# Multiplying the identity into an unread bank at the start of three attentions

## The reference

```python
x = x + tanh(g_xattn[l]) * xattn_l(layernorm(x), ctx)
x = x + tanh(g_ffn[l]) * ffn_l(layernorm(x))
# xattn_l, l = 1..3: q = x Wq + bq; k, v = ctx Wk + bk, ctx Wv + bv, by heads
# softmax(q k^T / 4) v, then Wo, bo.  Layer 0 has no projections, but a mask.
```

## Time and profile before

| | us |
|---|---|
| median of 3 runs | 1578.96 |
| lowest, highest | 1573.89, 1581.24 |
| the profiled execution, its own time | 1582.87 |
| its span, first to last instruction | 1581.1 |
| TensorE busy in it | 1334.4 (84%) |
| VectorE busy | 966.2 (61%) |
| mean granted TensorE clock | 0.920 |

### The profile page before, as it was taken

How to read it: one execution, slowest core, us unless ns; L and a number is a source line. 1 busy time by engine, 2 the same in 40 slices (tenths; PEclk the granted TensorE clock), 3 DMA queues, 4 the chain that set the end, 5 groups by cost and what they waited for, 6 DMA issues and landing times.

```text
span 1581.1 us, 29388 instructions
## 1 busy us (share of the span) xinstructions
PE 1334.4 (84%) x9497; PEld 967.6 (61%) x9524; DVE 966.2 (61%) x2651; ACT 861.4 (54%) x1718; POOL 722.0 (46%) x835
## 2 busy tenths in 40 slices
PE   1798889997999489999999699838999488995985
PEld 1455479854566279999986356627887245565433
DVE  6789753435795743333337489574554277877797
ACT  3366854433787145555536388535565255785564
POOL 4557330105641577777641473257994426523000
PEclk9999999996899699999999699968999797897998
DMA  9999120079970333343247997024544499930001
GB/s 296 289 135 138 12 97 1 27 234 189 113 85 1 107 124 121 118 137 131 71 151 257 227 133 83 14 81 134 159 133 170 159 269 161 120 45 1 0 14 40
DMA packets 142064, 188.86 MB, mean 119 GB/s; under 512 B 21168, under 2 KB 107824, under 8 KB 141872
## 3 DMA queue, kind: packets, MB, share of 16 engines
q0 software_dynamic: 79936, 105.19, 38.8%
q1 hardware_dynamic: 61984, 81.79, 16.1%
HBM read 128.17 MB, written 50.20 MB: 113 GB/s over the span
## 4 chain that ended last, share of the span: by engine, by line
PE 66%; DVE 13%; DMA 7%; ACT 5%; issue 5%; POOL 2%; another core or an unknown queue 0%; SPq 0%; ACTq 0%; DVEq 0%; POOLq 0%
PE PS L1191 10%; PE PS L1211 10%; PE PS L987 9%; PE PS L1032 9%; PE PS L991 3%; PE PS L1203 3%; DMA stack<-qk_parts 2%; PE PS L1069 2%; DMA qk_parts<-q_parts 2%; PE PS L1005 2%; PE PS L873 2%; PE PS L1045 2%; PE PS L1012 1%; PE PS L859 1%; DVE act L2572 1%
## 5 line engine op out<-in xcount | busy, mean ns | idle before, releaser
L2087 DVE TENSOR_REDUCE nm<-PS 128x2 f32<-128x512 f32 x384 | 250.4, 677 | 56.5 <-PE PS L987 55.7
L987 PE MATMUL PS<-stack 48*128 48x256 f32 x1024 | 221.7, 344 | 49.4 <-issue 15.9
L987 PEld LDWEIGHTS PS<-stack 48*128 48x128 f32 x1024 | 158.9, 214 | 137.9 <-issue 71.6
L991 PE MATMUL PS<-stack 49*128 49x256 f32 x1024 | 211.0, 331 | 0.9 <-ACT probs L1512 0.6
L1211 PE MATMUL PS<-weights,hh 128*128 x936 | 189.9, 292 | 3.8 <-DVE hl L2414 3.7
L1191 PE MATMUL PS<-weights,xh 128*128 x468 | 171.3, 421 | 10.7 <-DVE xl L2398 4.6
L662 POOL DMA_DIRECT2D stack<-mt x128 | 71.6, 559 | 227.0 <-ACT mt L1521 225.2
L1512 ACT ACTIVATE probs<-PS 128x512 f32<-128x512 f32 x256 | 145.1, 595 | 52.7 <-PE PS L991 24.0
L1512 ACT ACTIVATE xng<-PS 128x512 f32<-128x512 f32 x256 | 145.3, 595 | 28.4 <-PE PS L1012 14.9
L1211 PEld LDWEIGHTS PS<-weights,hh 128*128 128x128 f32 x936 | 152.7, 193 | 5.9 <-issue 5.5
L991 PEld LDWEIGHTS PS<-stack 49*128 49x128 f32 x1024 | 149.2, 203 | 10.1 <-ACT probs L1512 4.8
(11 more groups left out here) (329 smaller groups left out, 3091.6 us busy)
## 6 DMA issues: line engine op xcount, KB each, us to landing
stack<-qk_parts POOLq DMA_DIRECT2D x128, 256.0 KB, 4.9
qk_parts<-stack SPq DMA_DIRECT2D x32, 512.0 KB, 6.9
qk_parts<-q_parts SPq DMA_DIRECT2D x32, 512.0 KB, 9.5
stack<-qk_parts POOLq DMA_DIRECT2D x128, 128.0 KB, 4.1
weights<-W_dram POOLq DMA_DIRECT2D x12, 1024.0 KB
wide<-ctxT_dram SPq DMA_DIRECT2D x16, 512.0 KB, 7.7
wslot<-y_tokens SPq DMA_DIRECT2D x16, 512.0 KB, 7.5
weights<-W_dram POOLq DMA_DIRECT2D x12, 512.0 KB
```

What stands on the lines that cost most here:

```text
L987: mm = pe.matmul(PS[:, u % 3, to], nat_q[:, at], nat_k, start=True, stop=True)
L991: mm = pe.matmul(PS[:, 3 + v % 3, to], key_k[:, at], key_q, start=(l > 0 or half == 0), stop=(l > 0), skip_group_check=(l == 0))
L2087: nc.vector.tensor_reduce(nm[:, j % 2, at:at + 2], PS[:, (2 * t + h) % 3, :].rearrange("p (q n) -> p q n", q=2), AX.X, ALU.max, negate=Tru ...
```

## The change

In front of the attentions of layers 1 to 3 TensorE waits until the third group's query remainder has been taken (so that banks 6 and 7 have been read), and then multiplies the identity by 512 columns of `wproj` four times, into bank 7. Behind the scores of each of the first 16 units it does the same with 128 columns, once. Nothing reads the result, and nothing waits for it.

```diff
+FILLED = 16
...
             def attend(l):
 
+                if l:
+                    pe.wait_ge(qlo_done, GROUPS * (l + 1) - 1)
+                    idle(512, 4)
                 for n in range(QUADS + BACK):
                     for m in range(2):
                         units = [4 * n + 2 * m + h for h in range(2)]
                         keyed = [u - LAG for u in units]
                         for u, v in zip(units, keyed):
                             scores(l, u if u < HEADS * B else None, v if 0 <= v < HEADS * B else None)
+                            if l and u < FILLED:
+                                idle(P, 1)
...
+            def idle(n, times):
+
+                for _ in range(times):
+                    pe.matmul(PS[:, 7, 512 - n:], ident[:], wproj[:, 3].rearrange("p c n -> p (c n)")[:, 0:n], start=True, stop=True)
```

## The result

| | before | after |
|---|---|---|
| median, us | 1580.1 (4 runs) | 1599.2 (4 runs) |
| lowest, highest | 1573.9, 1583.5 | 1594.0, 1602.0 |
| profiled execution, its own time | 1582.9 | 1594.0 |
| mean granted clock in it | 0.920 | 0.929 |

The account below looks back on a forecast made before the run. It took TensorE's low clock at the attention starts of layers 1 to 3 as the loss: -8.6 us if held, -6.0 with layer 1 midway, -4.8 after late rows, 3 on the median: 1576 us, range 1567 to 1588.

Parts of the forecast that it names:

- The clock: Attention starts, layers 1 to 3: full at the first score, then held in layers 2 and 3, open in layer 1.
- the gap before unit 13: TensorE's wait for the first row of maxima, forecast to shrink to 1.4, 0.8 and 0 us in layers 1 to 3.
- the head: Four 512-column multiplications before the first score: 3.45 us, hidden in layers 1 and 3, first score 0.9 us later in layer 2.
- Units 13 to 19: Stage up to the first times-V block: 4.3 us with the clock held, gaining 0.8, 0.7 and 1.0 us.
- The unit: Each of units 0 to 15 with its filler: 0.76 us at full clock, 1.34 at low, over VectorE's 0.60.
- The neighbours: Steps around each score with a filler behind it: 0.23 us to its second half, 0.22 to the filler.
- The row: First row of maxima, issued 1.0, 2.2 and 1.0 us later; half counted as cost: 0.5, 1.1 and 0.5 us.
- The first reading: First row's transfer hangs on what is queued ahead, so it lands when it did: cost 0.
- a fixed latency: Other case for the first row's transfer: the whole shift of its issue counts, 1.0, 2.2 and 1.0 us.
- The low stretch behind the front: Low-clock time from the first times-V block on: 5.1, 1.6 and 1.5 us gained in layers 1 to 3 if held.
- The slower one: Rival: clock falls just behind unit 12 in every layer, units 13 to 15 cost 1.34 us each; 7.5 us, 1586; chance 0.17.
- the full gain: Rival: clock holds everywhere at the attention starts, little given back; -8.6 us or more, about 1570; chance 0.27.

Follow-up runs that it names:

- Experiment 5: Changed kernel with one 512-column bf16 multiplication as each filler and 26, 12, 20 of them before layers 1, 2, 3: 1573.66 us, ratio 0.998.
- experiment 3: Changed kernel with one bf16 multiplication of 512 columns replacing each float filler behind units 0 to 15, leading multiplications kept: 1587.96 us, ratio 1.0072.
- Experiment 8: Changed kernel with the same float fillers set in twos behind every second unit: 1577.24 us, ratio 1.0014.
- Experiment 1: Changed kernel without the fillers behind units 0 to 15, the four 512-column multiplications in front kept: 1576.0 us, ratio 1.0032.
- experiment 7: Changed kernel with fillers behind units 0 to 7 only, in place of sixteen units: 1583.19 us, ratio 1.0055.
- experiment 10: Changed kernel with bf16 multiplications: 26, 12, 20 in front, two behind every second unit to 11, twelve behind unit 12: 1568.13 us, ratio 0.9953.

## Why the prediction was wrong

**The clock (the step that failed).** The prediction says: "I take the clock as full when the first score starts", and lets it fall, if at all, in the gap before unit 13. It was full at the first score, and it fell under the fillers, 0.5, 5.5 and 5.4 us later, with TensorE busy without a pause from the first score on. In layer 1 the prediction's own figures warned of it: the head was to leave 4.85 - 3.45 = 1.4 us idle ahead of the first score and left 1.74, more than the 1.67 behind which it had seen the clock fall, but it asked this of the gap before unit 13 alone. In layers 2 and 3 no gap explains the fall; there the fillers, taken as work that holds the clock, did not hold it. How much hangs on it can be worked out. With the measured unit of 0.85 us and the clock held, units 0 to 12 with their three transposes take 13 x 0.85 + 0.33 = 11.4 us in place of 11.0, 10.8 and 9.6, gap included: 2.8 us more over three layers. They took 18.1 more. So, by this estimate, 15.3 of the stage's 18.1 us are the low clock. Units 13 to 19 add 6.2 where 2.5 were to be gained, for the same cause. Experiment 5, where the clock held in two of the three fronts, bears it out by taking back 24.7 us, 4.8 of them by its cheaper filler; within experiment 3 the one front that kept the clock took 18.3 us and the two that lost it 29.2 and 28.0.

**The unit (mis-sized term).** 0.76 us was forecast, 0.85 measured; at the low clock 1.34 and 1.44. The 0.11 us between two full-row instructions was read from back transposes, which are single instructions; the two halves of a float multiplication start 0.21 us apart at the full clock and 0.37 at the low one; at the full clock that is the whole of the miss. The term was small: 13 x 0.09 = 1.2 us a layer at the full clock, 0.10 us a unit at the low one. The prediction's estimate by the Trainium skill (TensorE: Matmul & The Clock Gate, What overlaps and what doesn't) was 0.86, and the trace agrees with it, at 0.85, though no run here separates the second weight load from the rest of its instruction.

**The neighbours (a term not seen).** A score was given 0.23 us for its second half and 0.22 to the filler, with no word of what it loses by no longer following another score. Experiment 8 prices that at 0.31 us of the 0.85. In the forecast's sum it was hidden in steps read from a stretch where single scores alternate with full-row work, so the sum came near; what it hid is that another order of the same instructions stays under VectorE's pace. The Trainium skill (same page and section) says that a weight load overlaps running multiplications only where their row groups differ. That full-row fillers shut the scores off from each other agrees with it, since a filler uses all rows: 0.85 us a unit with a filler behind each, 0.54 with two behind a pair.

**The row.** Forecast: issued 1.0, 2.2 and 1.0 us later, 0.9 of layer 2's being the head. Measured against the first score: 4.6, 1.7 and 1.3 us later. The 4.6 are the low clock of layer 1, and the 1.7 and 1.3 of layers 2 and 3 stand near the 1.3 and 1.0 of the forecast. Whether the landing moves with the issue, the prediction left open and took half; the DMA times settle it. Layer 1's first row, before and after:

```profile
DMA to landing us min/median/max: 6.4/6.4/6.4
...
DMA to landing us min/median/max: 1.7/1.7/1.7
```

In layers 2 and 3 it took 6.5 and 5.0 us before, 5.5 and 4.5 after. So it landed 10.9, 10.7 and 9.6 us behind the first score before, and 10.9, 11.4 and 10.4 after: the landing moved by 0, 0.7 and 0.8 us where the issue moved by 4.6, 1.7 and 1.3. The first reading (it hangs on what is queued ahead) is nearer than a fixed latency. None of it cost anything, as the row was there before TensorE reached unit 13 in all three layers.

**The low stretch behind the front.** Forecast for a held clock: 5.1, 1.6 and 1.5 us gained. It stayed low for 1.7, 3.4 and 6.6 us behind the first times-V block in place of 12.45, 3.78 and 3.75; 8.2 us less at 2.06 us in 5.00 are 3.4 us gained, by estimate, far less than the fillers cost.

**The head.** Right: near enough hidden in layers 1 and 3 (0.3 us more, 0.5 less), and 0.9 us later in layer 2 (3.96 us from the last query instruction to the first score, 3.09 before). Experiment 1 shows that it costs the fronts nothing and gains little.

**The rivals.** The slower one had the kind right (fillers that run at the low clock) and the place and size wrong: not behind unit 12 but from the first to the seventh unit on, and 25 us in the fronts in place of 7.5. The rule of the Trainium skill in the full gain (same page, Why this matters for your kernels), that TensorE kept busy reaches the full clock, did not hold here: layer 1 was busy for 27.82 of 27.82 us at a granted clock of 0.51. The prediction had set the 12.45 us busy and low of the earlier trace rows against that rule, and then let the fillers hold the clock anyway.

**What stays open.** Which property of the work lets the clock fall is not settled, and each kernel has one profiled execution. Where TensorE had not been idle ahead of the first score, single float fillers lost the clock 5.4 to 5.9 us behind it (layers 2 and 3 of the change, layer 2 of experiment 7), a transpose after 6.0, bare scores after 4.8 and 5.7. Single bf16 fillers held it through all 16 units in layer 2 of experiment 3 and layers 1 and 3 of experiment 5, and lost it after 10.6 us in layer 2 of experiment 5. Float fillers in pairs held it through units 0 to 12 in layers 2 and 3 of experiment 8, but not in layer 1, with 1.82 us idle ahead. The length of a gap doesn't decide alone either: the prediction had 0.98 us (stayed) and 1.67 (fell), but the clock fell behind 1.07 us in layer 1 of experiment 10 and stayed behind 1.36 us in layer 3 of experiment 5. Nor do the runs settle why the steady stage behind the fronts was faster in some executions.

## What to carry to other kernels

Before filler work is set between real instructions, take its unit cost at the low clock as well as at the full one, and ask who paces the stage: a filler that fits under VectorE's 0.60 us a unit costs nothing, one of 0.85 costs a little (by the estimate above 2.8 us over three layers), and the same one at 1.44 cost the fronts 25 us, where the full clock was forecast to give 8.6. Put fillers into waits and behind pairs, not between scores that overlap, and leave no gap between the filler work and the real work: that kernel was the only one here that was faster (0.9953). A rise of the mean granted clock is no gain by itself: here it rose from 0.920 to 0.929 and the kernel became 1.4% slower.

## What the runs showed of the hardware that was not expected

- A TensorE that never idles can lose the full clock and stay without it for 20 us and more: 27.82 us busy of 27.82 at 0.51 in the changed kernel, 17.05 of 17.05 and 17.28 of 17.28 at 0.50.
- Fillers of one kind and place don't hold the clock alike: one bf16 multiplication of 512 columns a unit kept 1.00 in layer 2 of experiment 3 (26 us) and in layers 1 and 3 of experiment 5, but not in layer 2 of experiment 5 (low after 10.6); a float one of 128 columns let it fall after 5.4 to 5.9, no later than bare scores.
- Two scores of 48 rows that follow each other, with both fillers behind them, take 0.62 us a unit; the same work with a filler behind each takes 0.85.
- The two halves of a 128-column float multiplication start 0.21 us apart at the full clock and 0.37 apart at the low one.
- The first row of maxima took 6.4 us from issue to landing in layer 1, and 1.7 us in the changed kernel, where it was issued 4.6 us later: it landed at the same distance from the first score.
